# Two heads' values in one 32-column tile of the probability products, in a two-layer attention and expert kernel

## The reference, cut to what matters

```python
scores = jnp.einsum('bhtc,bhsc->bhts', q, k) / math.sqrt(K_CH)
p_attn = jax.nn.softmax(scores, axis=-1)
out = jnp.einsum('bhts,bhsc->bhtc', p_attn, v)
out = out.transpose(0, 1, 3, 2).reshape(b, N_HEADS * K_CH, t_t)
```

## Time and profile before

| | us |
|---|---|
| median of 3 timed runs (lowest, highest) | 2049.42 (2048.53, 2051.22) |
| span of the profiled execution | 2053.3 |
| TensorE matmul busy | 1665.0 (81%) |
| TensorE weight load busy | 1127.2 (55%) |
| VectorE busy | 1414.6 (69%) |
| ScalarE busy | 1265.1 (62%) |
| GpSimd busy | 983.7 (48%) |

### The profile page before, as it was taken

How to read it: one execution, slowest core, us unless ns; L and a number is a source line. 1 busy time by engine, 2 the same in 40 slices (tenths; PEclk the granted TensorE clock), 3 DMA queues, 4 the chain that set the end, 5 groups by cost and what they waited for, 6 DMA issues and landing times. The chain is left out here.

```text
span 2053.3 us, 45004 instructions
## 1 busy us (share of the span) xinstructions
PE 1665.0 (81%) x12724; PEld 1127.2 (55%) x12879; DVE 1414.6 (69%) x4335; ACT 1265.1 (62%) x3302; POOL 983.7 (48%) x1114
## 2 busy tenths in 40 slices
PE   3999899999984999999998278888888888755551
PEld 1555555555543888888997134444444444444440
DVE  5888888888864455455433479999999999743331
ACT  1777677777761566666665268888888887721210
POOL 4367677777764000000000666666666662148883
PEclk9999999999996999999999589999999999979996
DMA  5689877777747976666665668888777775178856
GB/s 140 158 209 246 217 209 217 211 213 215 205 132 233 288 224 196 196 200 195 203 199 174 165 175 211 226 222 205 197 193 201 194 195 145 51 191 187 175 94 112
DMA packets 413088, 390.98 MB, mean 190 GB/s; under 512 B 46640, under 2 KB 385072, under 8 KB 412848
## 3 DMA queue, kind: packets, MB, share of 16 engines
q1 hardware_dynamic: 346496, 265.28, 48.8%
q0 software_dynamic: 37904, 90.22, 17.0%
q10 hardware_dynamic: 28448, 32.59, 5.5%
HBM read 233.74 MB, written 170.16 MB: 197 GB/s over the span
## 5 line engine op out<-in xcount | busy, mean ns | idle before, releaser
L1114 DVE TENSOR_REDUCE mx<-psS 128x2 f32<-128x512 f32 x1024 | 679.3, 675 | 100.4 <-PE psS L1507 66.8
L911 ACT ACTIVATE prob<-psE 128x512 f32<-128x512 f32 x1024 | 600.8, 594 | 226.0 <-PE psE L1520 209.2
L760 POOL DMA_INDIRECT yg<-y_d,row_all x256 | 248.7, 971 | 632.2 <-SPq L406 480.7
L1520 PE MATMUL psE<-q,k 128*128 128x256 bf16 x2048 | 394.7, 275 | 38.1 <-issue 15.9
L1507 PE MATMUL psS<-k,q 128*128 128x512 bf16 x869 | 336.5, 389 | 22.4 <-DMA k<-k_stack_d 12.8
L1630 PE MATMUL psE<-wt,xgT 128*128 (+1 forms) x1536 | 324.7, 335 | 2.0 <-ACT xgT L1010 1.6
L1459 DVE TENSOR_TENSOR hid<-sil,psE 128x96 f32<-128x96 f32 x384 | 97.8, 255 | 330.0 <-ACT sil L1015 329.8
L747 POOL DMA_INDIRECT xs_d<-xr,row_all x256 | 252.1, 985 | 111.0 <-ACT prob L911 67.6
L1520 PEld LDWEIGHTS psE<-q,k 128*128 128x128 bf16 x2048 | 185.6, 98 | 193.8 <-ACT prob L911 75.0
L1536 PE MATMUL psO<-prob,v 128*32 128x256 f32 x4096 | 275.9, 387 | 9.0 <-ACT osb L891 9.0
L1010 ACT COPY xgT<-psS 128x256 f32<-128x256 f32 x384 | 144.5, 376 | 187.1 <-PE psS L1624 170.2
(11 more groups left out here) (220 smaller groups left out, 2639.9 us busy)
## 6 DMA issues: line engine op xcount, KB each, us to landing
xg<-xs_d SPq DMA_DIRECT2D x320, 128.0 KB, 2.6
y_d<-y_all SPq DMA_DIRECT2D x320, 128.0 KB, 2.3
q<-q_stack_d SPq DMA_DIRECT2D x128, 256.0 KB
k<-k_stack_d SPq DMA_DIRECT2D x128, 256.0 KB
wt<-in_gu ACTq DMA_DIRECT2D x110, 192.0 KB, 3.3
q_stack_d<-parts SPq DMA_DIRECT2D x64, 192.0 KB
k_stack_d<-parts SPq DMA_DIRECT2D x64, 192.0 KB
wt<-in_dn ACTq DMA_DIRECT2D x110, 96.0 KB, 3.9
```

The lines of the kernel that those rows point to most:

```text
L760: g.indirect_dma_start(yg[:, k, :], None, y0_d[:, :], bass.IndirectOffsetOnAxis(row_all[:, row(st.pair("load") * K + k, 1)], 0))\
L911: a.activation(prob[gr][:, u % 4, :], psE[ring][:, :], ACT.Exp, scale=SCALE).then_inc(s_exp, 1)
L1114: v_.tensor_reduce(mx[b][:, bg // 4, :].rearrange("p (h r) -> p h r", h=2)[:, :, (bg % 4) * 2 + tt], psS[(UNITS * (st.s0 - LAG["smax"]) + ...
L1520: ins = m_.matmul(psE[ring][:, i * T:(i + 1) * T], k2[b][:, bg, hh * T + i * P:hh * T + (i + 1) * P], q2[b][:, bg, :], start=True, stop=True)
```

## The change

A quad's even-numbered and odd-numbered neighbours now share a result. The values of an even head stand in columns 0 to 8 of its 32-column tile, those of an odd head in columns 16 to 24 of its own, and each has zeros in the other's place. Two quads, one of even heads and one of odd heads, are added up in the same half of `psO`: the first starts the sum, the second ends it. So a pair has two results (`half` 0 and 1), not four: two copies out, at u = 12 and at u = 3 of the next step, and four transposes instead of eight. The units are taken in the order 0, 2, 4, 6, 1, 3, 5, 7, 8, 10, and so on. The number of matmuls of `values`, `scores` and `scores_t`, and of exponentials, stays.

```diff
-GROUPS = 4
+HALF = 16
+HALVES = 2
+def unit_at(u):
+    return 8 * (u // 8) + 2 * (u % 4) + (u % 8) // 4
...
-        osb = ab("osb", [P, GROUPS, T])
+        osb = ab("osb", [P, HALVES, T])
...
-            return tile[:, :].rearrange("p (h r) -> p h r", r=32)[:, :, o:o + n]
+            return tile[:, 0:2 * P].rearrange("p (h r) -> p h r", r=HALF)[:, :, o:o + n]
...
+        def ones_of(b, o):
+            to = v[b][:, 0, o, HALF * o + HC:HALF * o + HC + 1]
+            return bass.AP(to.tensor, to.offset, [list(to.ap[0]), [64, UNITS], [1, 1]])
...
-                    act.wait_ge(s_pv, st.n(stage, 4, q + 1))
-                    if q == 0:
+                    act.wait_ge(s_pv, st.n(stage, 4, 2 * half + 2))
+                    if half == 0:
                         wait(act, s_ot[1], last(st, stage))
-                    a.copy(osb[:, q, :], psO[:, (q % 2) * T:(q % 2 + 1) * T]).then_inc(s_oev, 1)
+                    a.copy(osb[:, half, :], psO[:, half * T:(half + 1) * T]).then_inc(s_oev, 1)
...
-                    if u == 0:
-                        o_out("back", 2)
                     if u == 3:
-                        o_out("back", 3)
+                        o_out("back", 1)
...
-                    if u == 8:
+                    if u == 12:
                         o_out("attn", 0)
-                    if u == 12:
-                        o_out("attn", 1)
...
-                        a.copy(v[b][:, :, :, 0:HC],
-                               psM[item_bank(L, "V")][:, 0:2 * P].rearrange("p (s h c) -> p s h c", s=2, c=HC))\
+                        to = v[b][:, 0, 0, 0:1]
+                        a.copy(bass.AP(to.tensor, to.offset, [list(to.ap[0]), [64, UNITS], [32 + HALF, 2], [1, HC]]),
+                               psM[item_bank(L, "V")][:, 0:2 * P].rearrange("p (h o c) -> p h o c", o=2, c=HC))\
...
-                v_.memset(v[b][:, :, :, 8:9], 1.0)
+                for o in range(2):
+                    v_.memset(ones_of(b, o), 1.0)
...
-                    b, bg, hh = st.buf("attn"), u // 2, u % 2
+                    b, bg, hh = st.buf("attn"), unit_at(u) // 2, unit_at(u) % 2
...
-                    wait(pe, s_oev, st.n(stage, 4, q))
+                    half, second = q // 2, q % 2
+                    if not second:
+                        wait(pe, s_oev, st.n(stage, 2, half))
                     for i in range(2):
                         for j in range(4):
-                            ins = m_.matmul(psO[32 * j:32 * j + 32, (q % 2) * T:(q % 2 + 1) * T],
-                                            v[b][:, i, 4 * q + j, :], prob[gr][:, j, i * T:(i + 1) * T],
-                                            start=(i == 0), stop=(i == 1))
+                            ins = m_.matmul(psO[32 * j:32 * j + 32, half * T:(half + 1) * T],
+                                            v[b][:, i, unit_at(4 * q + j), :], prob[gr][:, j, i * T:(i + 1) * T],
+                                            start=(i + second == 0), stop=(i + second == 2))
...
-                        product(f"OT{h}", "back", [(s_oev, st.n("back", 4))],
-                                [(osb[:, q, h * P:(h + 1) * P], None) for q in range(GROUPS)], s_ot[h])
+                        product(f"OT{h}", "back", [(s_oev, st.n("back", 2))],
+                                [(osb[:, half, h * P:(h + 1) * P], None) for half in range(HALVES)], s_ot[h])
```

More of the change, by code:

```diff
@@ L882, in body, with o_out @@
                 L = st.L
-                def o_out(stage, q):
+                def o_out(stage, half):
                     if not st.on(stage):
                         return
-                    act.wait_ge(s_pv, st.n(stage, 4, q + 1))
-                    if q == 0:
+                    act.wait_ge(s_pv, st.n(stage, 4, 2 * half + 2))
+                    if half == 0:
                         wait(act, s_ot[1], last(st, stage))
-                    a.copy(osb[:, q, :], psO[:, (q % 2) * T:(q % 2 + 1) * T]).then_inc(s_oev, 1)
+                    a.copy(osb[:, half, :], psO[:, half * T:(half + 1) * T]).then_inc(s_oev, 1)
                 def max_rows(stage, h):
```

## The result

The changed kernel takes 2036.34 us (median of 4 runs, 2035.62 to 2037.18), the kernel before, beside it on the same chip, 2048.98 us (median of 4, 2046.48 to 2051.22): a ratio of 0.9936, with a 95% interval of 0.9924 to 0.9949. It is 12.6 us faster, where 6.9 were forecast.

The account below looks back on a forecast made before the run. Layer 0 was taken as a round through VectorE, TensorE and ScalarE's copy at u = 8, layer 1 as VectorE almost alone. Gains of 6.3 and 0.6 us sum to 6.9, from 2049.4 to 2042.5 us; range 2035 to 2048.

Parts of the forecast that it names:

- The round of layer 0 passes ScalarE's copy: Layer 0, copy at u = 8: its removal gains 0.21 us a step, 6.3 us over 30 steps.
- the waits on this round: Layer 0: `scores_t(11)`'s weight load waits 0.2 us, not 0.43; VectorE's idle time before `red(12)` is 0.35, not 0.56.
- Nothing in layer 1's body: Layer 1's steps: VectorE almost alone makes the round, its two waits are on TensorE, so the removed copy gains 0.
- Four transposes at nothing: OT0 and OT1, both layers: four transposes fewer only lengthen TensorE's wait for `normalise(0)`, gain 0.
- the price in the open: Four transposes at 0.11 us each, 0.44 us a step; 28 us in all were nothing to hide them.
- the wait ahead of Q: TensorE's wait for `normalise(0)`: to grow from 0.52 to some 0.95 us in layer 0, 0.89 to 1.3 in layer 1.
- the cover: Work or waits hiding removed instructions: TensorE's wait for `normalise(0)` hides the transposes, VectorE's dense part the copy at u = 0.
- The ends of the layers, 0.6 us: End of layer 1's attention: quad 3 no longer 0.42 us late, OT0 0.22 us shorter, 0.6 us gained.
- At the end of layer 0 GpSimd's scatters are last, and I count nothing: End of layer 0: GpSimd's scatters finish last, so the change gains 0 there.
- Strides, the values' copy, the memsets at nothing: VectorE's stride-16 reads and the values' scattered copy taken at 0; doubled memsets ahead of the loops at 0 to 0.3 us.
- another case: Rival that TensorE bounds layer 0: transposes count each step, up to 14 us more gain, 2035 us; chance 0.11.
- S: Later theory: on chips with pauses the change is worth more, through the removed copy at u = 0 and quad 3's wait.

Follow-up runs that it names:

- the moves of VectorE: Changed kernel with `normalise(0)` ahead of `red(6)`: 0.9827 and 0.9832 of the kernel before; with `split_max` also ahead of `red(2)`: 0.9725 and 0.9779.
- the kernel with all work back: Changed kernel with both copies (u = 8 and u = 0, of a constant tile) and all eight transposes back, new layout and order kept: 2164.29 us, 1.0028 of before.

## Why the prediction was right, and where its size was off

1. *The round of layer 0 passes ScalarE's copy.* Right, in place and size: 17.17 us a step for 17.18, and the waits on this round moved as named (0.16 us for 0.2, 0.34 for 0.35). The copy put back alone returns 0.28 us a step in the same early steps that the change had cut by 0.28.
2. *Nothing in layer 1's body.* Right: 19.08 and 19.08, 0.5 us in 18 steps. The reason given, VectorE almost alone, was loose: it is a round of VectorE's work and its two waits, as the moves of VectorE show in one step.
3. *Four transposes at nothing.* Right for the body, and the price in the open, 0.44 us a step, was the prediction's own. But I had put all of the 0.44 us into the wait ahead of Q, which grew by 0.27 us in layer 0 and by 0.22 in layer 1. In layer 0 the step is itself 0.22 us shorter, so only 0.22 of TensorE's 0.44 could turn into idle time. In layer 1 TensorE idles some 0.5 us more a step, and most of that stands ahead of V: 0.82 us in a step of before, 1.45 in one of after. The term failed in where the cover ends.
4. *The ends of the layers, 0.6 us.* This is the mis-sized term. I priced the last quad of layer 1 alone. The table of stretches has 2.6 us there (1.6 + 1.0), 1.4 in the last two steps of layer 0 and 1.8 between the layers. In the last two steps of layer 1 each of the two removals counts in full, 0.31 and 0.44 us, as the kernels with the one or the other put back show. The trace of before had shown the cover going. TensorE's last projection of Q there, whose wait is the cover in every step before, starts at 1729.57 us, some ten us ahead of the last two steps (1739.80 to 1773.50).
5. *"At the end of layer 0 GpSimd's scatters are last, and I count nothing."* Wrong by those 1.4 and 1.8 us in the trace. No experiment took this place by itself, nor the 2.3 us in layer 1's first ten steps (where the clock differs too) and the 0.7 at the start. What caused them stays open.
6. *Strides, the values' copy, the memsets at nothing.* Right as far as shown: three durations unchanged to 4 ns, and the kernel with all work back at 1.0028 [0.9988, 1.0069].

The body gave 5.8 us (1.3 + 4.1, and two steps of 0.21 in the stretch of the half clock) against 6.3. The rest of the 12.6 is from beginnings and ends. Of it, the runs show some 1.5 us to be the change's (the last two steps of layer 1) and the rows 0.4 more (quad 3 at the end); the cause of the remainder is open. The stretches sum to 19.3 us, 14.7 without the row of the half clock; the 2 us above the timed gain are within the 4.7 by which the timed runs of before differ among themselves.

That the time fell within 2035 to 2048 us is in part luck. The gain of 12.6 us lies outside the 4.1 to 9 us to which the forecast itself gave 0.60. The low end of the range, 2035, had been set for another case, in which TensorE's transposes count in each step of layer 0; that case did not occur, and the ends of the layers, which the forecast put at 0.6 us, took its place.

## What to carry to other kernels

Follow one step round and name, for every removed instruction, the wait that now hides it; then do the same for the first and the last steps of each pipeline, where the stage that gave the cover does not run, and price it there in full. An engine at 75% can hold a step up while those at 94% and 89% wait for it, and one at 95% had a step cut by 0.29 us by moving one instruction ahead of another. Such a gain in one step is not yet one in the whole time: over the layer it was not there on the chips with pauses.

## What the runs showed of the hardware

On chips 7, 10 and 11 the same instructions last about as long as on the first (an exponential 598 and 591 ns in the mean, a `red` 677 and 674, in the changed kernel on chip 7 and on the first), but VectorE and ScalarE start later on TensorE's results. The step shown above from the first chip, at the same place in the changed kernel on chip 7:

```profile
1646.52 0.67 PE L1564 MATMUL psM<-xn,proj_q 128*128 128x256 f32 x2 [1.11 <-ACT xn L963]
1647.12 1.07 PE L1549 MATMUL psO<-prob,v 128*32 128x256 f32 x16
...
1650.00 0.69 DVE L1125 TENSOR_REDUCE mx<-psS 128x2 f32<-128x512 f32 x1 [1.99 <-PE psS L1518]
1650.04 0.60 ACT L923 ACTIVATE prob<-psE 128x512 f32<-128x512 f32 x1 [2.33 <-PE psE L1531]
```

From the quad to `red` it is 1.43 us on the first chip (1561.64 to 1563.07) and 2.88 here; to the exponential 1.65 and 2.92. The matmuls' starts are recorded at the same distances, but their ends are modelled. For each exponential, take its start less the later of two recorded ends, that of its matmuls and that of ScalarE's instruction before it. Over the 16 of a step this sums to 0.27 us in layer 0 and 0.16 in layer 1 on the first chip, and to 2.1 and 1.9 in the changed kernel on chip 7 (means over pairs 11 to 27), mostly at u = 6, 7, 8 and 12. It is 3.3 with the copy at u = 0 back, in layer 1. That kernel differs there in a second thing, the granted clock. Windows over the same 250 us, changed kernel and then the copy at u = 0 back, both chip 7:

```profile
1450.00:1700.00 250.00, 197.02 (x1742) 106.77 (x1774) 221.79 (x600) 187.90 (x441) 146.34 (x172) 1.00 0.72 182
```

```profile
1450.00:1700.00 250.00, 194.79 (x1591) 106.28 (x1618) 207.14 (x550) 175.79 (x414) 132.22 (x156) 0.92 0.66 168
```

The clock is 1.00 in the one and 0.92 in the other, stretches at its lower level of 1.2 GHz among those at 2.4. From pair 10 to 28 of layer 1 the kernel with the copy at u = 0 back takes 26.4 us more than the changed one. In the first 17 of these 18 steps, twelve hold such a stretch and take 22 to 23.4 us; the five without one take 19.8 to 21.1, where the changed kernel's are at some 20.5 and one holds a stretch. So the 26 us lie in the steps with a lower clock. Whether and how the copy brings these on isn't shown, and S's own reason, the pauses, can't be told apart from the clock here. The clock isn't all of it either: in the kernel with all work back, steps at a full clock take up to 22.0 us. What makes TensorE's results late on these chips is not settled. No run took the pauses away, and which way a change goes there can't be read from the recorded instructions alone.
